# Routing found chunk by chunk, graph scores taken from rows, and skip products, register loads and table loads moved, in a two-layer graph network on one core

## The reference, cut to what matters

```
# layer 0 experts, top 1
l = LN(x) @ Wr + br                    # 625 x 8
p = softmax(l); e = argmax(p)          # weight max(p), expert e
x += max(p) * FFN_e(LN(x))

# layer 1, graph attention k = 1, 2, 3
h = y @ W_k
s = h @ a_src ; d = h @ a_dst          # scores of a row
coef = softmax over neighbours of leaky_relu(s[src] + d[dst], 0.2)
out = leaky_relu(layer_norm(coef.T @ h + b + y @ Wsk_k + bsk))
```

## Time and profile before

| | |
|---|---|
| median of 3 runs | 1078.86 us (1078.42 to 1088.42) |
| the profiled execution | 1076.59 us, span 1074.8 us |
| PE busy | 980.3 us, 91% of the span |
| PEld, DVE, ACT, POOL busy | 638.2, 531.0, 399.3, 90.5 us |
| mean granted clock of PE | 0.958 of full speed |

### The profile page before, as it was taken

The page is one execution under the profiler, slowest core; times in us unless marked ns, Lnnn a source line. Parts: engine busy times, 40 slices in busy tenths (PEclk is TensorE's granted clock), DMA queues, the critical chain, the costliest instruction groups (busy, mean ns, idle before and its releaser), DMA issues. The chain is left out here.

```text
span 1074.8 us, 12489 instructions
## 1 busy us (share of the span) xinstructions
PE 980.3 (91%) x4831; PEld 638.2 (59%) x4831; DVE 531.0 (49%) x1111; ACT 399.3 (37%) x666; POOL 90.5 (8%) x83
## 2 busy tenths in 40 slices
PE   4888787999999999978999799999998799999998
PEld 1544442385454494468777565788998644445665
DVE  5668887433243411241211553287787634558561
ACT  3677675221102210011111322348886444332340
POOL 0000000000010202020000000034332000013000
PEclk9899998999998999968999899999999799999899
DMA  9489979750000104050672200412200400220001
GB/s 327 179 323 343 338 300 364 313 201 0 1 1 0 50 5 154 1 216 1 212 283 92 84 1 1 130 41 72 79 2 4 154 1 3 82 79 0 1 1 48
DMA packets 50646, 120.48 MB, mean 112 GB/s; under 512 B 4616, under 2 KB 18698, under 8 KB 50570
## 3 DMA queue, kind: packets, MB, share of 16 engines
q1 hardware_dynamic: 50042, 118.34, 30.4%
q10 hardware_dynamic: 528, 1.05, 0.3%
HBM read 118.10 MB, written 1.28 MB: 111 GB/s over the span
## 5 line engine op out<-in xcount | busy, mean ns | idle before, releaser
L386 PE MATMUL PS<-AR 128*125 128x512 f32 (+9 forms) x1514 | 437.8, 447 | 13.8 <-issue 7.0
L386 PEld LDWEIGHTS PS<-AR 128*128 128x128 f32 (+3 forms) x1514 | 236.0, 197 | 191.6 <-issue 183.1
L1778 ACT ACTIVATE AR<-PS 128x500 f32<-128x500 f32 (+6 forms) x71 | 40.9, 579 | 176.4 <-PE PS L386 85.4
L416 PE MATMUL PS<-AR 128*32 128x512 f32 x576 | 80.9, 619 | 24.3 <-DMA AR<-in_basis 24.3
L1781 ACT ACTIVATE AR<-iota,AR 125x625 f16<-125x625 f16 x119 | 86.6, 813 | 31.5 <-PE PS L470 31.4
L468 PE MATMUL PS<-AR 125*125 125x512 f16 (+9 forms) x425 | 61.8, 300 | 15.1 <-issue 9.0
L1186 DVE TENSOR_SCALAR AR<-iota,AR 125x625 f16<-125x625 f16 x165 | 60.6, 447 | 25.9 <-PE PS L470 25.8
L468 PEld LDWEIGHTS PS<-AR 125*125 125x125 f16 x425 | 45.4, 141 | 35.3 <-issue 27.4
L416 PEld LDWEIGHTS PS<-AR 128*32 128x32 f32 x576 | 18.7, 111 | 74.5 <-issue 51.0
L2243 POOL TENSOR_TENSOR whl<-AR,whh 128x512 fp32r<-128x512 f32 x32 | 46.7, 1480 | 90.0 <-ACT whh L1778 90.0
L1634 DVE TENSOR_TENSOR HMl<-AR,HMh 128x626 fp32r<-128x626 f32 x64 | 50.2, 825 | 5.3 <-ACT HMh L1778 5.3
(11 more groups left out here) (279 smaller groups left out, 1452.6 us busy)
## 6 DMA issues: line engine op xcount, KB each, us to landing
AR<-in_basis SPq DMA_DIRECT2D x80, 768.0 KB, 8.0
AR<-in_L_ffn_W SPq DMA_DIRECT2D x20, 1024.0 KB, 7.6
AR<-in_L_gnn_Wh SPq DMA_DIRECT2D x8, 512.0 KB, 3.9
AR<-in_L_gnn_Wh SPq DMA_DIRECT2D x16, 256.0 KB, 4.4
AR<-in_L_mix_W_qkv SPq DMA_DIRECT2D x1, 3072.0 KB, 11.2
AR<-in_L_gnn_root SPq DMA_DIRECT2D x2, 1024.0 KB, 14.5
AR<-in_WkvT SPq DMA_DIRECT2D x1, 2048.0 KB, 13.5
AR<-in_L_gnn_W SPq DMA_DIRECT2D x1, 2048.0 KB, 8.7
```

The lines of the kernel that those rows point to most:

```text
L386: ins = te.matmul(o, l, r, start=start and i == 0, stop=stop and i == len(pairs) - 1)
L416: ins = te.matmul(CB[32 * j:32 * j + 32, :], Am[:, l, m, 16 * (n % 2):16 * (n % 2) + 32], ring[:, at // 3, at % 3, :], start=m == quarter[ ...
L1778: return se.activation(o, i, ACT.Copy, scale=scale)
```

## The change

Five edits.

1. Routing runs per chunk. `logits(c)` goes to its own bank and releases DVE with `lg_full`; `route(c)` takes the maximum and its index from the logits, not from the softmax, and adds to `M`, `EM` and `G`. All copies of the transposes go to ACT. `logits(3)` comes before `turn2(4)`. The softmax (now only its top weight, as one over the sum of exponentials) is computed beside the place products.
2. `begin`: two register loads between the `xs` groups, six inside the experts' loop.
3. First attention: `h1` rows by a1s and a1d on DVE, then `spread`, as in the third attention. `mix_q(1, 0)` comes before it, and `mix_kv` before `coefs`.
4. Second attention: the skip products of chunks 0 and 1 are begun in slots 1 and 0 before the coefficients, and the slots are held.
5. `load_table` calls an activation on one column, so that the table's load comes there.

```diff
+            def logits(c):
+                read(psum["xt", 2, c])
+                if c > 1:
+                    pe.wait_ge(l0_read, c - 1)
+                chain(sl(2 + c % 2, 512, 520, P), [(XT[:, k, cols(c)], wr[:, k, :]) for k in range(4)]
+                      + [(ones[0:1, 0:P], brr[:, :])]).then_inc(lg_full, 1)
...
                 if c > 1:
-                    read(psum["xt", 2, c - 2])
-                    logits(c - 2, wr, brr[:, :])
+                    logits(c - 2)
+            logits(3)
             turn2(NT - 1)
-            for c in (3, 4):
-                read(psum["xt", 2, c])
-                ins = logits(c, wr, brr[:, :])
+            logits(4)
...
-            pe.wait_ge(em_ready, NT)
             u = psum.take("place", slot=3, incs=2)
             pe.wait_ge(pfx_ready, 1)
...
+                if k in (1, 2):                      # in the xs groups
+                    pe.wait_ge(off_ready, 2)
+                    begin.append(te.value_load(ioff[0:1, k - 1:k], min_val=0, max_val=N))
...
-            pe.wait_ge(off_ready, 2)
-            begin = [te.value_load(ioff[0:1, e:e + 1], min_val=0, max_val=N) for e in range(8)]
...
                 down(e)
+                if e < 6:
+                    begin.append(te.value_load(ioff[0:1, e + 2:e + 3], min_val=0, max_val=N))
                 if e:
                     back(e - 1)
...
-            scores(1, XT, 4)
             pe.wait_ge(d_mq, 16)
-            for m in range(4):
+            mix_q(1, 0, XT)
+            u = psum.take(("s", 1), "dve")
+            slot(u)
+            pe.wait_ge(row_score, 1)
+            spread(u, dsc)
+            for m in range(1, 4):
                 mix_q(1, m, XT)
             for c in range(NT):
+                mix_kv(1, c, XT)
                 coefs(1, c)
-                mix_kv(1, c, XT)
...
+            at2 = (1, 0)                             # after s2 (slot 2), d2 (slot 3), x1n (slot 0)
+            pe.wait_ge(d_w2, 32)
+            for c in range(2):
+                for s, v in psum.free[at2[c]]:
+                    pe.wait_ge(s, v)
+                for j in range(2):
+                    te.matmul(sl(at2[c], 512 * j, 512 * j + 512, P), x1a[:, cols(c)], W2C[:, 1024 + 512 * j:1536 + 512 * j],
+                              start=True, stop=False)
+            psum.held.update(at2)
...
             def a2(c):
-                u = psum.take(("a2", c), "act")
-                slot(u)
+                u = psum.take(("a2", c), "act", slot=at2[c] if c < 2 else None)
+                psum.held.discard(u.slot)
                 read(psum["y2", c])
+                own = [] if c < 2 else [(x1a[:, cols(c)], W2C[:, 1024 + 512 * j:1536 + 512 * j]) for j in range(2)]
...
+            def route(c):                            # DVE, called for c - 2 in chunk c, then for 3 and 4
+                dv.wait_ge(lg_full, c + 1)
+                lr, expert = sm[0:P, 0, c, :], sc[0:P, 3, c:c + 1]
+                ve.tensor_copy(lr, sl(2 + c % 2, 512, 520, P)).then_inc(l0_read, 1)
+                dv.wait_ge(l0_read, c + 1)
+                t = step(ve.max(sm[0:P, 3, c, :], lr))
+                dv.wait_ge(*t)
+                t = step(ve.max_index(smi[0:P, c, :], sm[0:P, 3, c, :], lr))
+                dv.wait_ge(*t)
+                t = step(ve.tensor_copy(expert, smi[0:P, c, 0:1]))
+                dv.wait_ge(*t)
+                ve.tensor_scalar(M[:, c, :], iota8[0:P, :], expert, None, ALU.is_equal)
...
+                ins = ve.scalar_tensor_tensor(out=G, in0=iota8[0:P, :], scalar=expert, in1=G, op0=ALU.is_gt, op1=ALU.add)
...
-            score_weights(1, lambda k: WC[:, 0, k, :], 4)
+            for c in range(NT):                      # DVE: h1 rows by a1s and a1d
+                row_scores(1, h1r, "h1", c)
+            on_diagonals()
+            mix_q(1, 0)
             scores(1)
...
+            def load_table(f):                       # ACT
+                act(zt[:, :], eps[:, :], f)
...
             for c in range(NT):
+                values(1, c, 1.0 / N)
                 if c % 2 == 0:
                     coefs_out(1, c)
-                values(1, c, 1.0 / N)
+            load_table(ACT.Sqrt)
...
+            load_table(ACT.Exp)                      # after the last head's gate
...
             exps(2, 4)
+            load_table(ACT.Sqrt)
             gathered(1)
```

More of the change, by code:

```diff
@@ L619, in _ @@
                     z_unit(1, r, kc)
[L621 to L625, removed]
+            def logits(c):
[4 more added lines that the diff above has]
+                      + [(ones[0:1, 0:P], brr[:, :])]).then_inc(lg_full, 1)
             def turn2(c):
                 pe.wait_ge(xn_ready, LN_L0 + c + 1)
-                turn(("xt", 2, c), c, XN, 4, "dve" if c % 2 else "act")
+                turn(("xt", 2, c), c, XN, 4, "act")
             for r in range(2):
@@ L798, in _ @@
             psum.held.discard(3)
-            def scores(l, xT, K):
-                u = psum.take(("s", l), "dve")
-                slot(u)
-                chain2(u.slot, [(wab[l][:, k, :], xT[:, k, :]) for k in range(K)]).then_inc(u.sem, 1)
-                u = psum.take(("d", l), "dve")
-                slot(u)
-                for c in range(NT):
-                    ins = chain(sl(u.slot, c, c + 1, P), [(xT[:, k, cols(c)], wa[:, 1, k:k + 1]) for k in range(K)])
-                ins.then_inc(u.sem, 1)
             def spread(u, d):
@@ L902, in _ @@
                     head_second(h - 1)
-            pe.wait_ge(wab_ready, 2)
+            pe.wait_ge(wab_ready, 1)
             pe.wait_ge(xa_ready, 1)
-            scores(2, x1a.unsqueeze(1), 1)
-            u = psum.take("x1n", "act")
+            u = psum.take(("s", 2), "dve", slot=2)
+            slot(u)
+            chain2(u.slot, [(wab[:, :], x1a)]).then_inc(u.sem, 1)
+            u = psum.take(("d", 2), "dve", slot=3)
+            slot(u)
+            for c in range(NT):
+                ins = te.matmul(sl(u.slot, c, c + 1, P), x1a[:, cols(c)], wa[:, 1, 0:1], start=True, stop=True)
+            ins.then_inc(u.sem, 1)
+            u = psum.take("x1n", "act", slot=0)
             slot(u)
@@ L1367, in _ @@
                         ve.tensor_scalar(MN[0:P, b, :], C[0:P, b, :], 0.0, BIG, ALU.is_equal, ALU.mult).then_inc(mn_ready, 1)
-                if c and c % 2 == 0:
-                    turned(("xt", 2, c - 1), c - 1, 4, XT)
+                if c > 1:
+                    before[0] = route(c - 2)
+            before[0] = route(3)
+            route(4)
             def softmax8(i, k):
@@ L1436, in _ @@
             ins.then_inc(dgk_ready, 1)
+            dv.wait_ge(soft_exp, 1)
+            t = step(ve.tensor_reduce(sc[0:P, 1, :], sm[0:P, 1, :, :], AX_X, ALU.add))
+            dv.wait_ge(*t)
+            top = step(ve.reciprocal(sc[0:P, 2, :], sc[0:P, 1, :]))
             for k in (1, 3):
@@ L1696, in _ @@
             for c in (2, 3, 4):
-                row_scores(c)
-            dv.wait_ge(*last[0])
-            for c in range(NT):
-                ins = ve.tensor_scalar(dsc[:, c, :], ident[0:P, 0:P], sc[0:P, 9, c:c + 1], None, ALU.mult)
-            ins.then_inc(row_score, 1)
+                row_scores(3, h3r, "h3", c)
+            on_diagonals()
             scores(3)
@@ L2225, in _ @@
                 ge.tensor_tensor(XL[:, c, :], XN[0:P, c, :], f32(XH[:, c, :]), ALU.subtract).then_inc(pool_xl, 1)
-            full("logits")
+            po.wait_ge(lg_full, NT)
             po.wait_ge(pool_xl, NT)
```

136 lines of the change are left out of this document (62 added, 74 removed).

## The result

The kernel after takes 1065.8 us (median of 19 runs, 1060.69 to 1073.49) against 1079.34 us for the kernel before (19 runs). The ratio is 0.9895, 95% interval 0.987 to 0.992: faster by about 1%, which is 11.3 us (8.6 to 14.0). The forecast was 1065.5 us, a gain of 13.4. The profiled execution took 1068.95 us, with a span of 1067.2 us, 7.6 us less than that of before, where 13.4 were forecast. The median agrees better than the trace and the ratio do, so the trace has to be read stage by stage.

The account below looks back on a forecast made before the run. PE's queue was taken to bound the kernel, busy 91% of the span. Terms -2.6 - 6.0 - 8.2 + 3.4 = -13.4 us gave a median of 1065.5 us, range 1058.5 to 1072.5.

Parts of the forecast that it names:

- Routing: Routing up to `place` and the gather: shorter wait after the last logits, less POOL's delay; gain 2.6 us, at most 3.5.
- POOL's hold on `route(4)`: Last routing chunk: three small DVE operations delayed beside POOL's XL operations; 1.5 us added, bounds 0 and 3.7.
- DVE operations of over 1 us in `route(4)`: Last routing chunk: listed as a sign that the forecast was wrong; no size of its own.
- Register loads: Before `up(0)`: the 3.43 us gap goes, gaining 3.4 us, and the clock stays up, 2.6 us more.
- Rival (c): Experts' loop: six register loads each drain PE and drop the clock; +5.4 us in all, 1084.3; chance 0.03.
- The bound of 7.8 us: Register loads: upper bound of the gain, if the second clock dip behind the expert biases goes too.
- First attention: First attention: score products replaced by one `spread` (7.4), clock dip gone (1.6), new wait before `a1` (0.85); gain 8.2 us.
- Rival (b): `up(0)` and `mix_q`: clock gains stay lost, and POOL fully blocks `route(4)`; total -7.0, 1071.9; chance 0.17.
- Rival (d): First attention: DVE's later scores set the pace, PE waits for numerators, 8 us given back; 1073.5; chance 0.04.
- Second attention: Second attention: early skip products cause slot waits and a clock drop; 3.4 us lost, from 0.5 to 6.
- Rival (a): Second attention: early skip products pay, slot pointer or clock behaving otherwise; gain 3.3 us, 1058.8; chance 0.15.
- The Sqrt table: Early square-root table calls in first and second attention: worth nothing, behind PE's work and the slot wait respectively.

Follow-up runs that it names:

- xh_early: Kernel of slots_moved with ACT's copies XH of chunks 0 to 3 ahead of its copy of the last transposes; ratio to the kernel before 0.9819.
- loads_back: Kernel after with only the register-load edit undone, all eight loads again ahead of `up(0)`; ratio to the kernel before 0.9941.
- early_jump: Kernel of slots_moved with PE's branch over the spare expert rounds taken once the last `back` is queued, not after it ends; ratio to the kernel before 0.9822.
- best: slots_moved plus xh_early, early_jump, order_table's coefficient order and another slot for the second attention's last coefficients, Exp table still called early; ratio to before 0.9816, median 1061.17 us.
- slots_moved: Kernel after with early skip products kept, but PSUM slots of `turn4(0)` and what follows chosen; ratio to the kernel before 0.9871.
- late_skip: Kernel after with the early skip products put back into `a2(0)` and `a2(1)`, no slot held, early table loads kept; ratio to the kernel before 0.9881.
- final: Kernel of best with XH back behind the last transposes and both early square-root table calls removed; ratio to the kernel before 0.9836.
- narrow_back: Kernel after with twenty chained one-column products (40 records) added behind the first attention's `spread`, results unread; ratio to the kernel before 0.9982.
- order_table: slots_moved with the first attention's last coefficients (and ACT's copies) ahead of its last keys and values, and no early Exp table call; ratio to the kernel before 0.9847.

## Why the prediction was right, and where it was not

- **Routing**, forecast -2.6 us: -2.4 and -2.2 up to `place` in the two profiles of after (11.76 and 11.97 us against 14.15, with the clock at 0.50 as assumed). POOL's hold on `route(4)` cost 0.8 + 1.1 = 1.9 us where 1.5 was taken; shown by xh_early. "DVE operations of over 1 us in `route(4)`" stood among the signs of being wrong, and they came (1.01 and 1.30 us). The sign was badly chosen, since the sum itself had a term for them.
- **Register loads**, forecast -3.4 and -2.6: the experts' stage is 2.5 us shorter, and that before it 2.5. Of the gap's 3.4 us about 1 went to the gather, where the clock came back later (0.50 at 482, against 0.88 in the earlier trace rows; 5.6 us at 0.50 from the gather's first product on, against 3.1). loads_back measured 5.8 to 6.0 us for the whole edit. The six loads in the loop cost nothing: between `up(0)` and the last `back` PE is idle once, for 1.50 us before that `back`, in both kernels. Rival (c) is out. The bound of 7.8 us asked for the second fall to go too; it did not go in after.
- **First attention**, forecast -8.2 behind the experts: -6.6 us from the last `back` to `xt4` (94.8 against 101.4). What went wrong is not a step that I wrote: the first transpose waited 7.36 instead of 4.14 us. In early_jump, where that wait is 4.14, the stretch takes 92.26 us, -9.1. The gain of the scores and the dip is thus a little above its range (6.5 to 9), and the extra wait costs 2.6 us of its 3.2 by `xt4`. The 0.98 us wait before `a1` was forecast at 0.85. Rival (b) is out as well, since the clock stood at 1.00 at 626 and `up(0)` took 3.74 us. Rival (d) is out: no coefficients waited for DVE.
- **Second attention**, forecast +3.4: +3.9 to `rows3(0)` and +0.8 to `skip(0)`, 4.7 in all. The slot wait was 3.79 us (forecast 3.7), `skip(0)`'s 0.69 (0.7), and `coefs(2, 4)` had its slot wait. The mis-sized terms are the clock and the saving. The clock already fell in the window at 844, behind the wait of `coefs(2, 4)`, so these coefficients took 2.16 instead of 1.33 us and the 32 products behind them 5.25 instead of 4.38 (as in best): 1.7 us. The skip products saved 3.4 us and not 3.7. slots_moved and late_skip confirm the mechanism by removing it. Rival (a), which read the rotation otherwise, is out for this choice of slots.
- **The Sqrt table** was right for this kernel only: it is worth nothing while `turn4(0)` waits for a later chunk, and 1.3 us of PE's wait once it does not (2.10 against 0.82 us, final and best).
- **What no term held**: the stage to the second attention's scores is 0.7 us longer and the last one 1.6 us shorter than before. The last stage of the kernel before has its clock at 0.56 and 0.59 from 994 to 998, and after has 1.00 in the same phase. In the stage to the scores after has a fall of the clock, from 716.9 to 720.3, and before has none. The code of these stages was hardly changed, and in other versions they vary between 130.9 and 133.6, and 151.4 and 154.3 us, with the number of falls, as said under the table. What places these falls is open.

Together: -13.4 forecast, -10.1 and -10.3 measured from the last addition on. By stage the errors are 0.2 (routing), 1.0 (loads), 1.6 (first attention), 1.3 (second) and -0.9 (stages without a term). The wait behind the experts, which no term held, is the largest single one. What each edit does was read rightly. That the medians differ by 13.5 us is in part luck: the ratio gives 11.3, and the stages 10.1 to 10.3.

## What to carry to other kernels

When work is issued early into a held buffer of a rotation, list who gets each buffer afterwards: here one free choice of slots turned an edit that lost 4.6 us into one that gains about 1.5. Compare versions between events around the edited stage, which repeated to 0.2 us in two profiles of one kernel, and not by whole runs, where the start of these stages moves by 6 us. Look at the granted clock of the stage first: one fall more or less goes with 0.7 to 1.6 us here, as much as most of these edits. Table calls, copies and small operations that are hidden by a wait must be judged again when that wait is removed.

## What was not expected of the hardware

- PE's wait behind a branch over unused code has two values, 4.0 to 4.1 and 7.2 to 7.6 us, in kernels whose PE code can be the same (best 4.14, final 7.64), and it goes with the start of one instruction packet of 0.02 MB: 1.5 to 1.7 us ahead of the last product in three of the four quick ones, 4.5 to 4.8 us behind it in the ten slow ones.
- The clock fell from 1.00 to 0.50 with PE busy all the time, during 40 one-column products (narrow_back), and in 11 of 13 profiles behind ten products 8 rows deep. In the two others (xh_early, early_jump) the same ten products left it at 1.00.
- An ACT_TABLE_LOAD sometimes starts as soon as ACT is free (824.82 in order_table, before the scores were ready at 825.39), and sometimes only with the data of its activation (848.55 in final, 4.16 us of idle ahead of it). Which of the two it will be could not be told from the kernel's text.
